# A sparse graph-attention layer: both adjacency searches together, GpSimd weights the own and row-aligned values, PE adds them

## The chip, the cores and the metric

The kernel runs on one core of a Trainium2 chip. The metric is the device time of one execution in microseconds (us), the median over runs. Before the change it is 662.41 us (3 runs, 660.38 to 662.70). A difference under about 0.5% (3.3 us) can't be told from no change. The engines are called PE (TensorE), DVE (VectorE), ACT (ScalarE), POOL (GpSimd) and SP (SyncE, which only issues transfers here).

## The reference

One layer of masked attention over N = 4096 rows of 256 features, 8 heads of 32, in float32, then a feed-forward block:

```python
mask = adj.astype(jnp.float32) + jnp.eye(n, dtype=jnp.float32)
q = (h @ Wq.T + bq).reshape(n, N_HEADS, D_K)      # k and v the same way
scores = jnp.einsum('nhd,mhd->hnm', q, k) / jnp.sqrt(jnp.float32(D_K))
scores = jnp.where(mask[None, :, :] == 0, jnp.float32(-1000000000.0), scores)
attn = jax.nn.softmax(scores, axis=-1)
ctx = jnp.einsum('hnm,mhd->nhd', attn, v).reshape(n, D_MODEL)
h1 = _layer_norm(h + ctx @ Wo.T + bo, ln1_g, ln1_b)
ff = jax.nn.relu(h1 @ W1.T + b1) @ W2.T + b2
return _layer_norm(h1 + ff, ln2_g, ln2_b)
```

`adj` is sparse, with few neighbours a row and more of them in the first tiles, so the kernel finds each row's neighbours and gathers only those. A second path (`general_*`), which is not run with these inputs, does the dense attention where a row has too many.

## The kernel before

The 4096 rows are 32 tiles of 128. A first phase (to about 98 us) projects keys and values into a table in HBM (`kv_table`) and starts on the queries. Then come 19 **steps**, numbered 0 to 18, in the order of `STEPS`. Steps 0 to 9, 17 and 18 take two tiles each (`q.T == 2`, one stretch of columns a tile, `q.nu == 1`). Steps 10 to 16 take one tile each, split into two or three stretches (`q.nu` 2 or 3). Tile 0, the densest, is done in pieces beside steps 2 to 14 (`TILE0`). Two steps make a group of four tiles (`place` 0 and 1), but steps 10 to 13 are one group and 14 to 16, with tile 0, another. The dense work of a group (output projection, feed-forward, both layer norms; `post_*`) runs one group later, spread over the gaps of the next group's steps.

A step works like this. DVE searches the adjacency rows of the step after the next with FIND_INDEX8 (`find_dve`, L492), once a tile. `listed_dve` and `spill_dve` (L505 to L533) turn what was found into lists. The first found column (or two) of a row is *row-aligned*: POOL gathers its key and value straight to that row's partition (L940). The rest are *edges*: PE and DVE sort them into shared chunks, and POOL gathers them (L948, and their queries, L952). A row's own key and value are loaded by SP. So each row has `q.own` slots in its own partition: 2 a tile in steps 0 to 5, 17 and 18, 3 in steps 6 to 9, 3 in steps 10 to 13 and 16, 4 in steps 14 and 15.

After the scores and the softmax (`norm_probs_dve`), the second half of a step has to be followed closely:

- DVE does the first search, takes a piece of tile 0 (L722), and subtracts the tops for the edges (`edge_below_dve`, L659).
- DVE multiplies the own and row-aligned values by their probabilities (L669 for two-tile steps, L672 and L675 for the others), and adds the slots into slot 0 (L682).
- DVE multiplies the edge values (`edge_weight_dve`, L688 and L691).
- PE sums into one PSUM bank (`sum_pe`): the edge chunks with a one-hot matrix (L822), and slot 0 with the identity (L823). ACT moves the result on (`ctx_act`), and the next group's projection (L998) waits for that.
- DVE does the second search (two-tile steps only), lists, spill, and at `place` 0 the second layer norm's statistics (L1083).

Each engine runs its own instructions in the order written; nothing is rescheduled. In that order PE's dense matmuls stand before and behind `sum_pe`, so whatever the sum waits for, they wait for too. At `place` 0, PE has the attention projection, then the queries of tile 0 (L835), and DVE's own piece of tile 0 (L702) waits for these.

Of the kernel before, what the change touches and what calls it, by code (L numbers as in the profile page):

```python
# [106 lines left out]
PIECES0 = TILE0.U // 2  # L107
SOFTMAX0 = SCORE0 + PIECES0
# [22 lines left out]
def build(nc, xT, adj, wqkvT, bq, bk, bqkv, woT, w1T, w2T, cols, g2, be2, out):  # L131
    with ExitStack() as ctx:
# [205 lines left out]
        own_sum = sem("own_sum")  # L338
        own_summed = sem("own_summed")
# [322 lines left out]
        def own_sum_dve(dve, q):  # L662
# [14 lines left out]
            dve.wait_ge(own_weighted, q.b + 1)  # L677
            done = total(lambda p: p.own - 1, q.b)
            v = slots[q.par][:, 0:q.T * q.own, D:].rearrange("p (t s) d -> p t s d", s=q.own)
            for a in range(1, q.own):  # L680
                wait(dve, own_sum, done + a - 1)
                nc.vector.tensor_tensor(v[:, :, 0, :], v[:, :, 0, :], v[:, :, a, :], ALU.add).then_inc(own_sum, 1)  # L682
# [125 lines left out]
        def sum_pe(pe, q):  # L808

            pe.wait_ge(edge_weighted, q.b + 1)  # L810
            wait(pe, own_sum, total(lambda p: p.own - 1, q.b + 1))
            pe.wait_ge(own_weighted, q.b + 1)
            wait(pe, ctx_ready, q.b)
            if q.b == SUM0 + 1:
                pe.wait_ge(ctx0_ready, 1)
            for ti in range(q.T):
                for k in range(KC):
                    to = ps[:, ACC, (k * 2 + ti) * P:(k * 2 + ti + 1) * P]
                    feats = slice(D + k * P, D + (k + 1) * P)
                    for u in range(q.nu):  # L820
                        c = ti * q.nu + u
                        nc.tensor.matmul(to, edge_slots(q)[:, c, feats], onehot[q.par][:, c, :], start=(u == 0), stop=False)  # L822
                    last = nc.tensor.matmul(to, own_slots(q, ti)[:, 0, feats], ident[:], start=False, stop=True)  # L823
            last.then_inc(acc_ps, 1)
# [79 lines left out]
        def ctx0_act(act):  # L904
# [4 lines left out]
            last.then_inc(ctx0_ready, 1)  # L909

# [449 lines left out]
        def _(pool):  # L1360
# [49 lines left out]
            for q in STEPS:  # L1410
# [11 lines left out]
                if soon:  # L1422
                    gather_edges(pool, soon)
                if 0 <= i - GATHER0 < PIECES0:
# [4 lines left out]
                if place == 1 and n >= 1:  # L1429

                    pool.wait_ge(edge_weighted, i + 1)
# [233 lines left out]
        def _(dve):  # L1665
# [42 lines left out]
            for q in STEPS:  # L1708
# [22 lines left out]
                if later:  # L1731
                    find_dve(dve, later, 0)
                if 0 <= i - SCORE0 < PIECES0:
# [6 lines left out]
                own_sum_dve(dve, q)  # L1740
# [5 lines left out]
                if later and later.T > 1:  # L1746
                    find_dve(dve, later, 1)
                if later:
# [55 lines left out]
```

## Time and profile before

| | before |
|---|---|
| median of 3 runs | 662.41 us |
| the profiled execution, its own time | 661.45 us |
| its span, first to last instruction | 659.4 us |
| PE busy (matmul) | 532.5 us, 81% |
| DVE busy | 477.9 us, 72% |
| POOL busy | 239.1 us, 36% |
| ACT busy | 169.6 us, 26% |
| mean granted clock of TensorE | 0.892 of 2.4 GHz |

The span leaves out 2.05 us around it (661.45 - 659.4). A PE row's duration is from issue to modelled end and matmuls overlap; the pace is read from start to start. "Idle before" names what ended an engine's wait, with its length.

### The profile page before, as it was taken

What the parts mean: (1) busy time and instruction counts of PE and PEld (TensorE: products, weight loads), DVE (VectorE), ACT (ScalarE), POOL (GpSimd) and SP (SyncE); (2) the same over time, 40 slices, a digit from 0 to 9 for tenths busy, and PEclk for the clock granted to TensorE, in tenths of its full rate; (3) what the DMA queues carried; (4) which work ended last, traced back from release to release, by engine and by line L of the source; (5) the groups of instructions that cost most, each with busy time, mean ns of one, the idle gap of its engine ahead of it and who ended that gap; (6) DMA issues with size and microseconds to landing.
All of it is one profiled execution on the core that took longest, in us unless ns stands there. A gap on an engine that the chain in (4) does not pass through costs nothing.

```text
span 659.4 us, 7652 instructions
## 1 busy us (share of the span) xinstructions
PE 532.5 (81%) x2434; PEld 423.7 (64%) x2434; DVE 477.9 (72%) x1210; ACT 169.6 (26%) x357; POOL 239.1 (36%) x370
## 2 busy tenths in 40 slices
PE   4999878884988897988889776588858489988891
PEld 3888667773577566747757652467755368577680
DVE  0798959869895997999779789989865996412000
ACT  1121312222421431342241242110314122521610
POOL 5010234454242373466424342424541424122222
PEclk9999778887899899889889986786959799999896
DMA  8999686997983888778562644347680843020100
GB/s 308 414 425 353 223 350 216 379 345 234 359 305 138 323 311 301 221 291 296 199 213 81 216 152 158 114 157 266 222 264 24 277 166 117 7 65 0 33 16 19
DMA packets 39211, 141.08 MB, mean 214 GB/s; under 512 B 4856, under 2 KB 15352, under 8 KB 35072
## 3 DMA queue, kind: packets, MB, share of 16 engines
q1 hardware_dynamic: 24320, 95.16, 39.1%
q0 software_dynamic: 13328, 43.55, 19.1%
q10 hardware_dynamic: 1520, 1.85, 0.8%
q8 instruction: 21, 0.34, 0.2%
q14 instruction: 22, 0.18, 0.1%
HBM read 123.74 MB, written 16.80 MB: 213 GB/s over the span
## 4 chain that ended last, share of the span: by engine, by line
PE 47%; DVE 29%; issue 8%; ACT 5%; DMA 5%; POOL 4%; POOLq 0%; SPq 0%; DVEq 0%; ACTq 0%
PE ps L1029 12%; PE ps L1017 12%; DVE found L492 7%; PE ps L1564 6%; PE ps L998 4%; DMA work<-q_table,row_of 4%; PE ps L988 3%; DVE stats L1083 2%; PE ps L822 2%; PE ps L823 2%; ACT early L1073 2%; ACT xT_all L1063 1%; DVE slots L682 1%; PE ps L864 1%; DMA xT_all<-in_xT 1%
## 5 line engine op out<-in xcount | busy, mean ns | idle before, releaser
L492 DVE FIND_INDEX8 found<-ones,adj_buf 128x8 uint32<-128x4105 int32 (+5 forms) x40 | 138.7, 3467 | 0.0
L1017 PE MATMUL ps<-xT_all,w 128*128 128x512 f32 (+1 forms) x288 | 129.6, 597 | 9.0 <-ACT xT_all L1063 7.9
L1029 PE MATMUL ps<-w,xT_all 128*128 128x256 f32 x512 | 123.7, 397 | 3.6 <-ACT xT_all L1063 3.1
L1029 PEld LDWEIGHTS ps<-w,xT_all 128*128 128x128 f32 x512 | 100.0, 200 | 18.2 <-ACT xT_all L1063 4.1
L1017 PEld LDWEIGHTS ps<-xT_all,w 128*128 128x128 f32 x288 | 57.3, 209 | 58.0 <-issue 45.0
L948 POOL DMA_INDIRECT slots<-kv_table,col_of x54 | 54.5, 1009 | 66.1 <-DVE col_of L566 54.5
L1083 DVE BATCH_NORM_STATS2 stats<-ps 128x6 f32<-128x256 f32 x64 | 22.9, 418 | 65.0 <-PE ps L988 65.0
L1564 PE MATMUL ps<-early,xT_all 128*128 128x256 f32 x256 | 59.1, 394 | 9.2 <-DMA xT_all<-in_xT 9.2
L1063 ACT ACTIVATE xT_all<-ps,col_table 128x512 f32<-128x512 f32 (+1 forms) x72 | 45.3, 641 | 71.3 <-PE ps L1017 66.8
L1564 PEld LDWEIGHTS ps<-early,xT_all 128*128 128x128 f32 x256 | 50.5, 199 | 16.5 <-issue 9.2
L822 PE MATMUL ps<-work,slots 128*128 128x128 f32 x160 | 35.5, 333 | 29.2 <-DVE slots L691 29.1
L940 POOL DMA_INDIRECT slots<-kv_table,found x32 | 33.6, 1051 | 56.8 <-PE ps L823 22.2
L1101 POOL TENSOR_TENSOR rstd<-mv,eps_col 128x4 f32<-128x4 f32 (+1 forms) x18 | 5.3, 297 | 132.5 <-DVE mv L1089 132.5
L822 PEld LDWEIGHTS ps<-work,slots 128*128 128x128 f32 x160 | 28.8, 238 | 33.4 <-DVE slots L691 33.4
L998 PE MATMUL ps<-wo,xT_all 128*128 128x256 f32 x128 | 36.8, 414 | 15.7 <-issue 12.4
L952 POOL DMA_INDIRECT work<-q_table,row_of x40 | 39.1, 978 | 12.2 <-issue 12.2
L892 ACT ACTIVATE xT_all<-ps,col_table 128x256 f32<-128x256 f32 (+1 forms) x38 | 14.4, 430 | 111.7 <-PE ps L823 111.7
L1582 PE MATMUL ps<-early,xT_all 128*128 128x256 f32 x128 | 38.0, 425 | 0.0
L1110 POOL TENSOR_TENSOR early<-early,row_g 128x1024 f32<-128x1024 f32 (+1 forms) x9 | 19.0, 2109 | 49.5 <-DVE slots L691 43.9
L998 PEld LDWEIGHTS ps<-wo,xT_all 128*128 128x128 f32 x128 | 24.0, 209 | 18.4 <-issue 16.2
L785 PE MATMUL ps<-idx_all,work 128*128 128x9 f32 (+1 forms) x80 | 12.9, 273 | 24.5 <-DVE work L547 24.5
L1582 PEld LDWEIGHTS ps<-early,xT_all 128*128 128x128 f32 x128 | 28.1, 219 | 5.0
(165 smaller groups left out, 881.3 us busy)
## 6 DMA issues: line engine op xcount, KB each, us to landing
adj_buf<-in_adj SPq DMA_DIRECT2D x31, 2048.0 KB
xT_all<-in_xT SPq DMA_DIRECT2D x15, 512.0 KB, 21.4
kv_table<-slots POOLq DMA_DIRECT2D x7, 1024.0 KB, 11.4
slots<-kv_table SPq DMA_DIRECT2D x12, 512.0 KB
q_table<-slots POOLq DMA_DIRECT2D x16, 256.0 KB, 9.5
out_dram<-early SPq DMA_DIRECT2D x7, 512.0 KB
q_own<-q_table SPq DMA_DIRECT2D x12, 256.0 KB
slots<-in_adj SPq DMA_DIRECT2D x1, 2048.0 KB, 24.5
```

The lines of the kernel that those rows point to most:

```text
L492: last = nc.vector.max_index(dst, ones8[:], part)
L822: nc.tensor.matmul(to, edge_slots(q)[:, c, feats], onehot[q.par][:, c, :], start=(u == 0), stop=False)
L940: nc.gpsimd.indirect_dma_start(to, None, kv_dram, bass.IndirectOffsetOnAxis(ap=idx, axis=0)).then_inc(got_aligned[q.par], 16)
L948: nc.gpsimd.indirect_dma_start(edge_slots(q)[:, u, :], None, kv_dram, bass.IndirectOffsetOnAxis(ap=col_of[q.par][:, u:u + 1], axis=0)).the ...
L952: nc.gpsimd.indirect_dma_start(q_edge[q.par][:, u, :], None, q_dram[q.no // 2], bass.IndirectOffsetOnAxis(ap=row_of[q.par][:, u:u + 1], ax ...
L998: nc.tensor.matmul(to, q["ctxT"][:, k, j * P:(j + 1) * P], wo[:, k, :], start=(k == 0), stop=False)
L1017: last = nc.tensor.matmul(ps[:, q["bank"] + f % 2, 0:q["g"] * P], w1[:, k, f * P:(f + 1) * P], q["h1T"][:, k, :], start=(k == 0), stop=(k ...
L1029: nc.tensor.matmul(to, q["ffT"][:, f, j * P:(j + 1) * P], w2[:, f, :], start=(f == 0), stop=False)
L1063: nc.scalar.activation(q["ffT"][:, f, :], ps[:, q["bank"] + f % 2, 0:q["g"] * P], ACT.Relu, bias=bias_1[:, f:f + 1]).then_inc(q["ff"], 1)
L1083: last = nc.vector.bn_stats(q["stats"][k][:, j, :], tile_out(q, q["bank"] + 2 * k, j))
L1564: last = nc.tensor.matmul(ps[:, kv_bank(i, part), j * D:(j + 1) * D], xT_all[:, c, k, r * P:(r + 1) * P], wqkv[:, k, (1 + part) * D:(2 + p ...
L1582: last = nc.tensor.matmul(to, xT_all[:, c, k, r * P:(r + 1) * P], wqkv[:, k, 0:D], start=False, stop=(k == KC - 1))
```

## The change

From step 2 on (`OWN_BY_POOL = 2`), the weighting of the own and row-aligned values moves from DVE to POOL (`own_weight_pool`), behind POOL's gathers for the next step and ahead of its gathers for tile 0. In all 19 steps the adding of the slots on DVE (L682) is gone: PE accumulates each slot with the identity, which makes `q.own` matmuls where there was one, for each tile and half of the features. In steps 2 to 18 DVE does the second search right behind the first, and the lists and spill ahead of the edge weighting, where they were behind it. POOL's gain and bias of the second layer norm (L1110, L1114) no longer wait for the step's edge weighting.

```diff
-        def own_sum_dve(dve, q):
+        def own_weight_dve(dve, q):
 ...
             last.then_inc(own_weighted, 1)
-            dve.wait_ge(own_weighted, q.b + 1)
-            done = total(lambda p: p.own - 1, q.b)
-            v = slots[q.par][:, 0:q.T * q.own, D:].rearrange("p (t s) d -> p t s d", s=q.own)
-            for a in range(1, q.own):
-                wait(dve, own_sum, done + a - 1)
-                nc.vector.tensor_tensor(v[:, :, 0, :], v[:, :, 0, :], v[:, :, a, :], ALU.add).then_inc(own_sum, 1)
 ...
             pe.wait_ge(edge_weighted, q.b + 1)
-            wait(pe, own_sum, total(lambda p: p.own - 1, q.b + 1))
             pe.wait_ge(own_weighted, q.b + 1)
 ...
-                    last = nc.tensor.matmul(to, own_slots(q, ti)[:, 0, feats], ident[:], start=False, stop=True)
+                    for a in range(q.own):
+                        last = nc.tensor.matmul(to, own_slots(q, ti)[:, a, feats], ident[:], start=False, stop=(a == q.own - 1))
 ...
+        def own_weight_pool(pool, q):
+
+            pool.wait_ge(own_probs, q.b + 1)
+            for ti in range(q.T):
+                v = own_slots(q, ti)[:, :, D:].rearrange("p s (h d) -> p s h d", d=DK)
+                if q.nu == 1:
+                    p = score_tiles(q)[:, ti, 0:q.own, :]
+                    last = nc.gpsimd.tensor_tensor(v, v, p.unsqueeze(3).to_broadcast([P, q.own, HEADS, DK]), ALU.mult)
 ...
+            last.then_inc(own_weighted, 1)
 ...
                 if soon:
                     gather_edges(pool, soon)
+                if i >= OWN_BY_POOL:
+                    own_weight_pool(pool, q)
 ...
                 if place == 1 and n >= 1:
-
-                    pool.wait_ge(edge_weighted, i + 1)
                     pool.wait_ge(s_weights, 16 * WEIGHT_DMAS)
 ...
                     find_dve(dve, later, 0)
+                if i >= OWN_BY_POOL and later and later.T > 1:
+                    find_dve(dve, later, 1)
 ...
                 edge_below_dve(dve, q)
-                own_sum_dve(dve, q)
+                if i < OWN_BY_POOL:
+                    own_weight_dve(dve, q)
+                elif later:
+                    listed_dve(dve, later)
+                    spill_dve(dve, later)
                 edge_weight_dve(dve, q)
 ...
-                if later and later.T > 1:
+                if i < OWN_BY_POOL and later and later.T > 1:
                     find_dve(dve, later, 1)
-                if later:
+                if i < OWN_BY_POOL and later:
                     listed_dve(dve, later)
                     spill_dve(dve, later)
```

On DVE, the second half of a two-tile step (step 3), before (MAX_INDEX is what the trace calls FIND_INDEX8; `adj_buf0` and `adj_buf1` hold the two tiles that are searched):

```order
L492 MAX_INDEX found<-ones8,adj_buf0 128x8
L659 TENSOR_TENSOR p_edge<-s_edge,ps 128x16
L669 TENSOR_TENSOR slots<-slots,scores 128x2x256 x2
L682 TENSOR_TENSOR slots<-slots 128x2x256
L688 SCALAR_TENSOR_TENSOR p_edge<-p_edge,ps 128x16
L691 TENSOR_TENSOR slots<-slots,p_edge 128x2x256
L492 MAX_INDEX found<-ones8,adj_buf1 128x8
L505 CAST idx_all<-found 128x2x8
L518 TENSOR_TENSOR mask1<-idx_all,limit 128x16
L520 TENSOR_REDUCE spill<-mask1 128x2
L526 SCALAR_TENSOR_TENSOR idx_all<-idx_all,row_ids 128x8 x2
L529 TENSOR_SCALAR half<-spill 128x2
```

and of the change, the same place:

```order
L492 MAX_INDEX found<-ones8,adj_buf0 128x8
L492 MAX_INDEX found<-ones8,adj_buf1 128x8
L659 TENSOR_TENSOR p_edge<-s_edge,ps 128x16
L505 CAST idx_all<-found 128x2x8
L518 TENSOR_TENSOR mask1<-idx_all,limit 128x16
L520 TENSOR_REDUCE spill<-mask1 128x2
L526 SCALAR_TENSOR_TENSOR idx_all<-idx_all,row_ids 128x8 x2
L529 TENSOR_SCALAR half<-spill 128x2
L531 SCALAR_TENSOR_TENSOR mask1<-idx_all,mask1 128x16
L533 TENSOR_SCALAR mask1<-mask1 128x16
L682 SCALAR_TENSOR_TENSOR p_edge<-p_edge,ps 128x16
L685 TENSOR_TENSOR slots<-slots,p_edge 128x2x256
```

The second search and the list work (L505 to L533) stand ahead of the edge weighting (L688 and L691, now L682 and L685); the own weighting and the adding are gone from DVE.

On POOL, step 5, from the gathers of the edges of step 6 to the next aligned gathers, before:

```order
L948 DMA slots<-kv_table,col_of 128x512
L952 DMA work<-q_table,row_of 128x256
L948 DMA slots<-kv_table,col_of 128x512
L952 DMA work<-q_table,row_of 128x256
L948 DMA slots<-kv_table,col_of 128x512 x2
L1110 TENSOR_TENSOR early<-early,row_g 128x1024
L1114 TENSOR_TENSOR early<-early,row_be 128x1024
L940 DMA slots<-kv_table,found 128x512 x4
```

and of the change:

```order
L960 DMA slots<-kv_table,col_of 128x512
L964 DMA work<-q_table,row_of 128x256
L960 DMA slots<-kv_table,col_of 128x512
L964 DMA work<-q_table,row_of 128x256
L914 TENSOR_TENSOR slots<-slots,scores 128x2x256 x2
L960 DMA slots<-kv_table,col_of 128x512 x2
L1122 TENSOR_TENSOR early<-early,row_g 128x1024
L1126 TENSOR_TENSOR early<-early,row_be 128x1024
L952 DMA slots<-kv_table,found 128x512 x4
```

Two multiplications (L914) stand between the next step's gathers and tile 0's, and the gain and bias are L1122 and L1126.

On PE, the sum of a step with three slots a tile (step 6), before:

```order
L822 MATMUL ps<-work,slots 128x128
L823 MATMUL ps<-ident,slots 128x128
L822 MATMUL ps<-work,slots 128x128
L823 MATMUL ps<-ident,slots 128x128
L822 MATMUL ps<-work,slots 128x128
L823 MATMUL ps<-ident,slots 128x128
L822 MATMUL ps<-work,slots 128x128
L823 MATMUL ps<-ident,slots 128x128
```

and of the change:

```order
L815 MATMUL ps<-work,slots 128x128
L817 MATMUL ps<-ident,slots 128x128 x3
L815 MATMUL ps<-work,slots 128x128
L817 MATMUL ps<-ident,slots 128x128 x3
L815 MATMUL ps<-work,slots 128x128
L817 MATMUL ps<-ident,slots 128x128 x3
L815 MATMUL ps<-work,slots 128x128
L817 MATMUL ps<-ident,slots 128x128 x3
```

One identity matmul becomes three for each tile and half.

## Rows read from the trace of the kernel before

**Rows 1.** the page: span, and the chain of waits by engine
```profile
span 659.4 us, 7652 instructions
PE 47%; DVE 29%; issue 8%; ACT 5%; DMA 5%; POOL 4%; POOLq 0%; SPq 0%; DVEq 0%; ACTq 0%
```

**Rows 2.** groups by line of PE (count | busy us, mean ns | idle before)
```profile
L822 PE MATMUL ps<-work,slots 128*128 128x128 f32 x160 | 35.5, 333 | 29.2 <-DVE slots L691 29.1
...
L823 PE MATMUL ps<-ident,slots 128*128 128x128 f32 x124 | 28.3, 316 | 0.0
...
L797 PE MATMUL ps<-work 128*128 128x56 f32 (+1 forms) x80 | 11.6, 271 | 3.1 <-DVE work L590 3.0
```

**Rows 3.** timeline of PE, steps 4 and 5 (start us, us, engine, line, operation, count, idle)
```profile
218.93 0.49 PE L822 MATMUL ps<-work,slots 128*128 128x128 f32 x2 [1.88 <-DVE slots L691]
...
248.10 0.39 PE L822 MATMUL ps<-work,slots 128*128 128x128 f32 x2
...
249.89 0.28 PE L778 MATMUL ps<-spill,minus_before 128*128 128x2 f32 x2
```

**Rows 4.** timeline of DVE, step 4, and step 5's last weighting
```profile
204.31 0.69 DVE L702 TENSOR_TENSOR slots<-ps,slots 128x512 f32<-128x512 f32 x1 [6.44 <-PE ps L835]
...
216.06 0.68 DVE L669 TENSOR_TENSOR slots<-slots,scores 128x512 f32<-128x512 f32 x1
...
217.38 0.69 DVE L682 TENSOR_TENSOR slots<-slots 128x512 f32<-128x512 f32 x1
...
218.87 4.43 DVE L492 FIND_INDEX8 found<-ones,adj_buf 128x8 uint32<-128x4105 int32 x1
...
224.51 0.42 DVE L1083 BATCH_NORM_STATS2 stats<-ps 128x6 f32<-128x256 f32 x1
...
242.90 0.69 DVE L691 TENSOR_TENSOR slots<-slots,p_edge 128x512 f32<-128x512 f32 x1
```

**Rows 5.** timeline of DVE, step 8: weighting and adding with three slots a tile
```profile
328.45 1.82 DVE L669 TENSOR_TENSOR slots<-slots,scores 128x768 f32<-128x768 f32 x2
...
330.30 1.42 DVE L682 TENSOR_TENSOR slots<-slots 128x512 f32<-128x512 f32 x2
```

**Rows 6.** timeline of PE: the sum's first matmul in steps 2, 8 and 15
```profile
164.44 0.58 PE L822 MATMUL ps<-work,slots 128*128 128x128 f32 x1 [4.56 <-DVE slots L691]
...
332.58 0.54 PE L822 MATMUL ps<-work,slots 128*128 128x128 f32 x1 [2.08 <-DVE slots L691]
...
516.35 0.58 PE L822 MATMUL ps<-work,slots 128*128 128x128 f32 x1 [5.00 <-DVE slots L691]
```

**Rows 7.** timeline of PE: waits behind a sum, steps 7, 12, 16
```profile
287.32 0.70 PE L1017 MATMUL ps<-xT_all,w 128*128 128x512 f32 x1 [2.34 <-ACT xT_all L1063]
...
426.44 0.50 PE L785 MATMUL ps<-idx_all,work 128*128 128x9 f32 x3 [1.85 <-DVE work L547]
...
521.65 0.38 PE L778 MATMUL ps<-spill,minus_before 128*128 128x2 f32 x2 [1.53 <-DVE spill L520]
...
526.48 0.50 PE L785 MATMUL ps<-idx_all,work 128*128 128x9 f32 x3 [1.85 <-DVE work L547]
```

**Rows 8.** one line's instructions (ns min/median/max, first and last start, forms): L1110, L511
```profile
L1110 POOL TENSOR_TENSOR early<-early,row_g x9: 1262/2350/2354, 243.7 to 648.1; 128x1024 f32<-128x1024 f32 x7, 128x512 f32<-128x512 f32 x2
...
L511 DVE CAST aligned_idx<-idx_all x7: 168/170/2341, 332.6 to 483.9; 128x2 uint32<-128x2 f32 x5, 128x3 uint32<-128x3 f32 x2
```

**Rows 9.** timeline of GpSimd: step 5's last gather, step 9's gain
```profile
241.33 0.95 POOL L948 DMA_INDIRECT slots<-kv_table,col_of  x1 [0.30 <-issue]
...
358.39 2.35 POOL L1110 TENSOR_TENSOR early<-early,row_g 128x1024 f32<-128x1024 f32 x1 [5.58 <-DVE slots L691]
```

**Rows 10.** timeline of DVE in step 9: the cast
```profile
358.43 2.34 DVE L511 CAST aligned_idx<-idx_all 128x2 uint32<-128x2 f32 x1
```

**Rows 11.** timelines at step 17: GpSimd's last gather, PE's first sum matmul
```profile
558.71 0.95 POOL L952 DMA_INDIRECT work<-q_table,row_of  x1 [0.30 <-issue]
...
560.54 0.39 PE L822 MATMUL ps<-work,slots 128*128 128x128 f32 x2
```

More of the change, by code:

```diff
@@ L107 @@
 PIECES0 = TILE0.U // 2
+OWN_BY_POOL = 2
 SOFTMAX0 = SCORE0 + PIECES0
@@ L337, in build @@
         own_weighted = sem("own_weighted")
-        own_sum = sem("own_sum")
-        own_summed = sem("own_summed")
         edge_weighted = sem("edge_weighted")
@@ L909, in ctx0_act @@
             last.then_inc(ctx0_ready, 1)
+        def own_weight_pool(pool, q):
[5 more added lines that the diff above has]
+                    last = nc.gpsimd.tensor_tensor(v, v, p.unsqueeze(3).to_broadcast([P, q.own, HEADS, DK]), ALU.mult)
+                else:
+                    p = score_tiles(q)[:, ti, 0:1, :]
+                    last = nc.gpsimd.tensor_tensor(v[:, 0:1], v[:, 0:1], p.unsqueeze(3).to_broadcast([P, 1, HEADS, DK]), ALU.mult)
+                    if q.A:
+                        p = unit_scores(q, 0, 1)[:, :, 0, :]
+                        last = nc.gpsimd.tensor_tensor(v[:, 1:], v[:, 1:], p.unsqueeze(3).to_broadcast([P, q.U, HEADS, DK]), ALU.mult)
+            last.then_inc(own_weighted, 1)
         def tables_ready(eng, q):
```

## The prediction

> **What bounds the kernel now.** I read the page first, then PE's groups by line, then the timelines of PE and DVE side by side, step by step. The chain of waits gives PE 47% and DVE 29% of a span of 659.4 us [rows 1]: two engines take turns. PE's sum is where they meet. Its first matmul follows 29.1 us of waiting for DVE's edge weighting, over 19 steps [rows 2], and its dense work is queued behind it. The reader is to see which steps hold that wait. They are the steps at place 0 (2, 4, 8 and 10) and three of the later, one-tile ones (11, 14, 15); four of them stand in [rows 3, 6]. At place 1 it is the other way round: in step 5 DVE has ended its weighting at 243.6 (242.90 + 0.69), and PE comes to the sum at 248.10 [rows 3, 4], 4.5 us of slack.
>
> So a pair of steps runs like this. From the end of a sum at place 1, PE goes through ctx and projection to L835; DVE waits 6.44 us for that, starts at 204.31, and has a fixed chain of its own up to the sum at 218.93. Then PE is full until 249.9. Work taken from DVE helps only inside that chain of 14.6 us. Elsewhere DVE would wait longer for PE.
>
> **The change part by part.** All sums are made against the profiled execution (661.45 us, of which 659.4 are the span and 2.05 lie around it). It stands 0.96 us under the median of 662.41.
>
> *PE's added matmuls.* One matmul in the program is two rows here: 124 rows of L823 for 62 calls [rows 2]. From 248.10 to 249.89 stand the 16 rows of one sum, 0.112 us each [rows 3]. The change adds 8 rows in a step with two tiles and two slots, 16 with two tiles and three slots (steps 6 to 9), 8 with one tile and three slots, 12 in steps 14 and 15. That is 192. The first 16 fall in steps 0 and 1, where the next step waits for gathers, and I count them nothing (if that cover is gone, 1.8 us). The other 176 by 0.112 are 19.7 us. They stand right behind the wait, ahead of everything that PE and ctx do next, in an engine that is full; I take all. The floor is half of it, if waits further on absorb the rest; the ceiling is twice it, 39 us, with the clock at the lower of its two levels (1.2 for 2.4 GHz) throughout.
>
> *The sum comes later where the second search is put ahead of it.* In step 4 the search and lists take from 218.87 to 224.51 (5.64, with its load 5.75) [rows 4]. What goes is the own weighting and adding, 216.06 to about 217.99 (1.93; the last add starts at 217.38). So the edge weighting ends 3.8 us later. In step 2 it is the same, in step 6, with three slots, the part that goes is 1.82 + 1.42 = 3.24 [rows 5], so 2.5 later, and in step 15 (four slots) about 3.1. These are steps where PE already waits for DVE or arrives with it (4.56, 1.88 and 5.00 us of waiting in 2, 4 and 15 [rows 3, 6]), so the delay goes straight on: 3.8 + 3.8 + 2.5 + 3.1 = 13.2 us. In steps 3, 5, 7 and 16 the 4.5 us of slack, as in step 5, hide it, with under 1 us left. The bounds of this term are 10 and 17.
>
> *GpSimd as the last.* POOL's price for a float32 product is not in this trace at these shapes with this broadcast. The nearest rows are 1.26 us for 512 elements and 2.35 for 1024 [rows 8]. I take 1.27 for 512, 1.8 for 768, 0.65 for 256. From below it is DVE's 0.69 for 512 [rows 4], from above twice the row. The work waits in POOL's order behind four to six gathers of 1.25 us each, and starts some 4 us after the probabilities. Beside two searches (9 us) that is hidden even at the upper price. Beside one it isn't: in steps 8, 10 and 14 DVE would reach the sum 1 to 2 us sooner, but POOL ends about when DVE ended before. And in step 17, where nothing is left to search, POOL's last gather ends at 559.66 and its products need 2.5 us more, against 560.54 for PE's sum [rows 11]: 1.6 us late.
>
> *The two engines hold each other up.* In step 9 the cast at 358.43 takes 2.34 us, beside GpSimd's gain (L1110), which starts at 358.39 and takes 2.35 [rows 9, 10]. Line L511 otherwise takes 0.17 [rows 8]. So small DVE work that falls beside a POOL product waits for its end, while the searches beside POOL are not slowed. With the wait on the edge weighting gone, the gain and bias in steps 5, 7, 9 and 15 start behind own weighting and tile 0's gathers. In step 5 the last gather is at 241.33 [rows 9]; 2.5 us more for the products, and gain and bias run from 245 to 250. DVE's lists now stand there, from 245.1 on, ahead of the edge weighting. It would end at about 251.2 where 247.4 was due, and PE's slack is gone: 2.9 us late. In steps 7, 9 and 15 the same arithmetic gives 0 to 2.8, 0 to 1.5 and 0 to 2.3, depending on tenths; I take 2.5 for the three. With steps 8, 10 and 14 (list work beside own weighting, 2.3 together, of 0 to 4) and step 17's 1.6 this term is 2.9 + 2.5 + 2.3 + 1.6 = 9.3 us, bounds 2 and 14.
>
> The Trainium skill ("SBUF — State Buffer", on the port pair that DVE and GpSimd share) says that a DVE instruction with two SBUF inputs, or in a two-port mode, and a GpSimd instruction that reads SBUF exclude each other for their full length. The trace agrees, with 2.34 against 0.17 us. By that rule edge weighting can also hold POOL up, 0.69 us at a time; the sum does not use this.
>
> *Given back.* With lists ahead of the sum, what DVE did between the sum and the next step is gone, and waits behind the sum close: L797's 3.0 us (steps 12 and 13 [rows 2]), 1.85 in step 12, 1.53 and 1.85 in step 16, and 2.34 in step 7, where the statistics now stand right behind the edge weighting [rows 7]. That is 10.6. Step 11, whose list work is shorter than the adding that goes, gives 0.8. Together 11.4 us; at least 6, at most 15.
>
> The sum: 19.7 + 13.2 + 9.3 - 11.4 = 30.8. 661.45 + 30.8 = 692.25; I predict **692 us**.
>
> **The rivals.**
>
> *GpSimd is hidden and the collisions don't happen.* The gain waits for the norm of ACT, which the later sum may delay, and then it would start beside PE's waiting and not beside the lists. For it: three of four collisions hang on tenths. Against it: the statistics stand earlier, so the norm is ready. Then 9.3 falls to about 1.6: 684.5 us.
>
> *GpSimd is much slower.* The product reads a broadcast in the innermost dimension, L1110 one in an outer. At twice the row, POOL's part in steps 8 to 10, 13, 14 and 17 grows by 3.6 or less each, 12 us together: 704 us. For it: no row has this form. Against it: nothing in the rows.
>
> *The searches wait for adjacency.* The second search is 7 us earlier against its own load. DVE never waits for it now. If it did by 3 us in four steps, it would be 704 as well.
>
> *Faster: DVE sets the pace.* If the chain of 29% on DVE were what bounds the pairs, the freed work (1.9 us in most steps, 3.2 in four) would shorten them. The point that decides is the sum's wait in steps 8, 10, 11 and 14: with GpSimd ready before DVE, each would shrink by up to 2 us, 6 to 8 together. For a faster kernel the added matmuls would also have to run in PE's waits, and the second search would have to be hidden in 2, 4 and 15. Then 661.45 - 7 = 654 us. Against it: PE waits only 1.88 us in step 4 and 4.56 in step 2, and DVE waits 6.44 for PE.
>
> *The delay is absorbed.* The change does what it says, but PE's extra rows and later sums vanish in waits: no change, 661 to 664.
>
> **How the numbers follow.** My forecast has 0.60 and its own range is 684 to 700. Hidden GpSimd has 0.20, slow GpSimd or late adjacency 0.14 together, absorbed 0.03, faster 0.03. The range of 8 in 10 takes in 684.5 and reaches down for the floor of the matmul term (9.9 less) and up toward 704: 674 to 704. About 0.5%, 3.3 us, can't be told from no change, and every case but the last two is far above it: slower 0.94, same 0.03, faster 0.03.
>
> **What would show it.** Right: PE's sum has 24 or 32 rows, with 0.112 us from one to the next at the full clock; the wait ahead of the sum in steps 2 and 4 grows by 3.8 us and more; DVE's wait at L835 grows beyond 6.44; L505 or L526 in step 5 takes about 2 us beside GpSimd's gain; DVE's busy time falls while the span grows. Wrong: PE's waits ahead of the sum stay as they were, products at GpSimd that take twice 1.27 us, a search that waits for its load, or a span under 674 us.

## The result and the profile after

| | before | changed |
|---|---|---|
| median, in one comparison on one chip | 662.56 us (4 runs) | 701.61 us (4 runs) |
| ratio | | 1.064, 95% interval 1.060 to 1.069 |
| the profiled execution, its span | 661.45, 659.4 us | 700.09, 698.3 us |
| granted clock of TensorE, mean of the span | 0.892 | 0.887 |

Slower, as forecast, but by 38.6 us from one profiled execution to the other where 30.8 were worked out, and by 6.4%, about 42 us, as the ratio has it. The median lies in the range of 674 to 704, and above the forecast's own 684 to 700; 662.41 times the ratio is 705, just above both.

The ratio is taken from fast executions only, side by side (one of the four before, at 667.24 us, was slow; without it their median is 662.41). It isn't the quotient of the medians, which is 1.059 here. In the runs below the two differ by up to 7 thousandths, 5 us, so a difference between two ratios is known to no better than that.

The page of the changed kernel: span, busy time and the chain of waits.

```profile
span 698.3 us, 7969 instructions
...
PE 557.4 (80%) x2626; PEld 450.6 (65%) x2626; DVE 454.3 (65%) x1144; ACT 169.3 (24%) x357; POOL 272.2 (39%) x404
...
PE 45%; DVE 35%; issue 6%; DMA 5%; ACT 4%; POOL 3%; SPq 0%; POOLq 0%; DVEq 0%; ACTq 0%
```

DVE's busy time fell from 477.9 to 454.3 us, and its share of the chain rose from the 29% of [rows 1] to 35%: less work, but more of it where PE waits. PE's groups by line (the sum is now L815 and L817) say the same:

```profile
L817 PE MATMUL ps<-ident,slots 128*128 128x128 f32 x316 | 55.6, 318 | 0.0
...
L815 PE MATMUL ps<-work,slots 128*128 128x128 f32 x160 | 35.9, 334 | 50.8 <-DVE slots L685 50.1
```

Against [rows 2], 192 rows came as counted (124 to 316), and the sum's wait for the edge weighting grew from 29.1 to 50.1 us. Step 4, DVE's timeline (start us, us):

```profile
211.38 0.69 DVE L696 TENSOR_TENSOR slots<-ps,slots 128x512 f32<-128x512 f32 x1 [5.68 <-PE ps L829]
...
218.52 4.43 DVE L492 FIND_INDEX8 found<-ones,adj_buf 128x8 uint32<-128x4105 int32 x1
...
222.93 4.43 DVE L492 FIND_INDEX8 found<-ones,adj_buf 128x8 uint32<-128x4105 int32 x1
...
229.05 0.69 DVE L685 TENSOR_TENSOR slots<-slots,p_edge 128x512 f32<-128x512 f32 x1
```

and PE's:

```profile
229.79 0.79 PE L815 MATMUL ps<-work,slots 128*128 128x128 f32 x2 [5.67 <-DVE slots L685]
```

From DVE's piece of tile 0 to the sum it is 18.41 us (211.38 to 229.79), where [rows 3, 4] had 14.62 (204.31 to 218.93): 3.8 us, the forecast to the tenth. DVE's own wait for L829 (L835 before) is 5.68 us, though, where the prediction named growth beyond 6.44 as a sign of being right. And in step 6, where 2.5 us and the rows' 1.8 were forecast, the kernel falls back by another 8.2, from 14.8 us behind at the end of step 5 to 23.0. Some 4.1 of them lie ahead of the sum. The rest is in the length of the sum itself. Step 6, the sum of the changed kernel:

```profile
288.74 0.61 PE L1000 MATMUL ps<-ident,early 128*128 128x128 f32 x4
293.42 0.79 PE L815 MATMUL ps<-work,slots 128*128 128x128 f32 x2 [4.07 <-DVE slots L685]
294.01 1.49 PE L817 MATMUL ps<-ident,slots 128*128 128x128 f32 x6
295.29 0.63 PE L815 MATMUL ps<-work,slots 128*128 128x128 f32 x2
295.71 1.49 PE L817 MATMUL ps<-ident,slots 128*128 128x128 f32 x6
...
299.53 3.60 PE L1029 MATMUL ps<-xT_all,w 128*128 128x512 f32 x8
```

Its 32 rows take 6.11 us (293.42 to 299.53), 0.19 us each, and not the 0.112 that stands in the prediction; before, its 16 rows took 1.89. The same stretch by windows (busy us of each engine with its rows, granted clock, DMA share, GB/s). The second row is the wait, the third the sum, the fourth the next projection:

```profile
core 0: us, PE busy (x) PEld busy (x) DVE busy (x) ACT busy (x) POOL busy (x), PEclk, DMA share, GB/s
...
274.00:289.00 15.00, 12.95 (x69) 11.51 (x68) 13.56 (x31) 2.25 (x5) 8.01 (x10) 0.89 0.27 65
289.40:293.40 4.00, 0.00 (x0) 0.00 (x0) 3.86 (x14) 1.55 (x3) 1.93 (x2) 0.79 0.98 406
293.40:299.50 6.10, 6.08 (x32) 6.08 (x33) 3.20 (x11) 0.00 (x0) 1.91 (x4) 0.58 0.99 418
299.50:306.00 6.50, 6.50 (x21) 3.49 (x20) 2.69 (x6) 4.36 (x9) 3.86 (x4) 1.00 0.85 306
```

PE stood idle for 4 us, the granted clock fell, and the sum ran at 0.58, most of it at 1.2 GHz. The next 6.5 us are at 2.4 GHz again. The Trainium skill ("TensorE: Matmul & The Clock Gate", on how the oscillation bites in real kernels) tells of this pattern: a wait for data lets the clock down, and the stage behind the wait starts at the low rate every time. The trace agrees here, 0.58 against 1.00, but not for "every time": in step 7 the sum's 32 rows take 5.30 us behind 3.13 us of waiting, and in a second trace of the same kernel (below) 3.68 us behind 3.16.

The collision of GpSimd with the lists in step 5, DVE:

```profile
256.53 1.50 DVE L505 CAST idx_all<-found 128x16 f32<-128x16 uint32 x1
...
258.35 2.26 DVE L526 SCALAR_TENSOR_TENSOR idx_all<-idx_all,row_ids 128x8 f32<-128x8 f32 x2
```

and POOL beside it:

```profile
251.14 2.06 POOL L914 TENSOR_TENSOR slots<-slots,scores 128x512 f32<-128x512 f32 x2
...
255.62 2.36 POOL L1122 TENSOR_TENSOR early<-early,row_g 128x1024 f32<-128x1024 f32 x1
258.06 2.38 POOL L1126 TENSOR_TENSOR early<-early,row_be 128x1024 f32<-128x1024 f32 x1
```

The cast ends about when L1122 ends (257.98), L526 about when L1126 does (260.44), as L511 did in [rows 9, 10]. 1.50 and 2.26 stand where 0.17 and 0.36 do in step 4, 3.2 us together.

### The profile page after: what moved, and what is told of

Its sections match the earlier page's. It is cut to its first block, busy times and chain, and to the rows that moved or that the text cites. A ratio compares the mean times of both kernels' runs of the same rounds, so it can differ in the third digit from the quotient of the medians.

```text
span 698.3 us, 7969 instructions
## 1 busy us (share of the span) xinstructions
PE 557.4 (80%) x2626; PEld 450.6 (65%) x2626; DVE 454.3 (65%) x1144; ACT 169.3 (24%) x357; POOL 272.2 (39%) x404
## 4 chain that ended last, share of the span: by engine, by line
PE 45%; DVE 35%; issue 6%; DMA 5%; ACT 4%; POOL 3%; SPq 0%; POOLq 0%; DVEq 0%; ACTq 0%
DVE found L492 13%; PE ps L1029 10%; PE ps L1041 7%; PE ps L1576 6%; PE ps L817 6%; PE ps L1010 5%; DMA work<-q_table,row_of 4%; PE ps L815 4%; PE ps L1000 3%; DVE stats L1095 2%; DVE slots L685 1%; DMA xT_all<-in_xT 1%; ACT early L1085 1%; POOL slots L960 1%; PE ps L858 1%
## 5 line engine op out<-in xcount | busy, mean ns | idle before, releaser
L1029 PE MATMUL ps<-xT_all,w 128*128 128x512 f32 (+1 forms) x288 | 126.8, 588 | 5.7 <-ACT xT_all L1075 4.6
L815 PE MATMUL ps<-work,slots 128*128 128x128 f32 x160 | 35.9, 334 | 50.8 <-DVE slots L685 50.1
L815 PEld LDWEIGHTS ps<-work,slots 128*128 128x128 f32 x160 | 29.1, 239 | 55.6 <-DVE slots L685 54.6
L952 POOL DMA_INDIRECT slots<-kv_table,found x32 | 33.2, 1037 | 79.9 <-PE ps L817 50.7
L1576 PEld LDWEIGHTS ps<-early,xT_all 128*128 128x128 f32 x256 | 50.5, 198 | 16.6 <-issue 9.3
L817 PE MATMUL ps<-ident,slots 128*128 128x128 f32 x316 | 55.6, 318 | 0.0
L1010 PE MATMUL ps<-wo,xT_all 128*128 128x256 f32 x128 | 40.9, 450 | 15.9 <-issue 10.2
L817 PEld LDWEIGHTS ps<-ident,slots 128*128 128x128 f32 x316 | 50.8, 235 | 0.0
L964 POOL DMA_INDIRECT work<-q_table,row_of x40 | 38.0, 950 | 12.2 <-issue 12.2
L1010 PEld LDWEIGHTS ps<-wo,xT_all 128*128 128x128 f32 x128 | 26.0, 225 | 19.1 <-issue 14.5
L539 DVE SCALAR_TENSOR_TENSOR bad<-spill,ps 128x2 f32<-128x2 f32 (+2 forms) x20 | 3.1, 154 | 52.5 <-PE ps L772 52.5
```

Source lines behind the costliest of these rows:

```text
L817: last = nc.tensor.matmul(to, own_slots(q, ti)[:, a, feats], ident[:], start=False, stop=(a == q.own - 1))
L964: nc.gpsimd.indirect_dma_start(q_edge[q.par][:, u, :], None, q_dram[q.no // 2], bass.IndirectOffsetOnAxis(ap=row_of[q.par][:, u:u + 1], ax ...
L1010: nc.tensor.matmul(to, q["ctxT"][:, k, j * P:(j + 1) * P], wo[:, k, :], start=(k == 0), stop=False)
L1029: last = nc.tensor.matmul(ps[:, q["bank"] + f % 2, 0:q["g"] * P], w1[:, k, f * P:(f + 1) * P], q["h1T"][:, k, :], start=(k == 0), stop=(k ...
L1576: last = nc.tensor.matmul(ps[:, kv_bank(i, part), j * D:(j + 1) * D], xT_all[:, c, k, r * P:(r + 1) * P], wqkv[:, k, (1 + part) * D:(2 + p ...
```

## The experiments

Each ran beside the kernel before on one chip; the ratio is to that, with its 95% interval. Beside it stands the lag, how much later than in the profiled kernel before PE began its first row behind a sum, from trace to trace (us). "Waits filled" means unread matmuls ahead of PE's waits; they come below.

| kernel | ratio | step 1 | 2 | 4 | 6 | 8 | 11 | 15 | 18 |
|---|---|---|---|---|---|---|---|---|---|
| changed | 1.064 | 4.3 | 8.2 | 12.9 | 23.0 | 29.1 | 34.7 | 37.0 | 40.0 |
| search behind | 1.008 | 5.0 | 4.7 | 4.8 | 6.2 | 5.5 | 7.9 | 5.4 | 5.5 |
| PE's added rows alone | 0.999 | 2.5 | 2.5 | 0.8 | 1.9 | -0.5 | 2.9 | -3.3 | -1.7 |
| order alone | 1.049 | -0.5 | 3.5 | 11.1 | 19.8 | 19.6 | 21.0 | 24.1 | 27.1 |
| order alone, waits filled | 1.030 | -0.3 | 2.2 | 8.1 | 15.0 | 12.9 | 12.8 | 15.7 | 20.1 |
| changed, waits filled | 1.028 | 4.5 | 6.8 | 9.6 | 17.4 | 20.2 | 20.8 | 23.6 | 25.4 |
| before, waits filled | 1.005 | -0.5 | -3.6 | -5.7 | -5.6 | -6.6 | -4.8 | -8.9 | -7.2 |
| all three taken away | 1.017 | -0.4 | 1.8 | 6.2 | 9.7 | 9.1 | 10.3 | 11.7 | 14.9 |

**PE's added rows alone.** The order of before, DVE weights, and PE adds the slots, in all steps. The edit is shown against the changed kernel.

```diff
-OWN_BY_POOL = 2
+OWN_BY_POOL = NB
+                    pool.wait_ge(edge_weighted, i + 1)     # gain
```

> The kernel before, but PE adds the slots (192 more matmul rows) and DVE no longer does; weighting, searches and the gain's wait stay where they were. Ledger theory (each term as in the prediction, waits absorb rows where PE waits for DVE): the rows cost their full 0.112 us each only in the steps where PE comes last (3, 5, 7, 9, 12, 13, 16 to 18), and nothing in steps where DVE's add (0.7 to 1.4 us) goes away ahead of the sum: about +12 us, 674. Rival, every added row lies on the path: +19.7 us, 682. Rival, the lower clock behind waits makes rows dearer than 0.112: over 682.

Measured: 657.77 us, 0.999 (0.994 to 1.003), at a clock of 0.926. The 19.7 us of the prediction are not there. DVE is rid of its adding, the sum's wait falls from 29.1 to 20.4 us,

```profile
L815 PE MATMUL ps<-work,slots 128*128 128x128 f32 x160 | 32.0, 305 | 20.4 <-DVE slots L685 20.4
```

and PE runs more of the time at its high level. So the rows are there and yet cost nothing: PE's busy time is 534.4 us for 532.5, although 192 rows by 0.112 are 21.5. The rest of its work got shorter by nearly as much. Two waits that the prediction took as given back by the order are gone here too, with the order of before: L797's 3.0 us in steps 12 and 13, and most of the 2.34 us in step 7 (0.56 are left).

**The order alone.** The kernel before with only the second search, lists and spill ahead of the edge weighting, from step 2 on.

```diff
+                if i >= 2 and later and later.T > 1:
+                    find_dve(dve, later, 1)
...
                 own_sum_dve(dve, q)
+                if i >= 2 and later:
+                    listed_dve(dve, later)
+                    spill_dve(dve, later)
```

> The kernel before with only the order of DVE changed from step 2 on: second search right behind the first, lists and spill ahead of the edge weighting; DVE still weights and adds, PE has no more rows. Ledger theory: the weighting ends 5.75 us later in steps 2, 4, 6 and 15, about 1.2 later in one-tile steps, 1 to 2 us over the slack in 3, 5 and 7, and 10 us are given back: about +20 us, 682. If the longer waits of PE also lower its granted clock: +24 or more, 686 to 692, with a mean clock under 0.887. Rival, the order is harmless and the rows of PE are all of the loss: 662.

Measured: 690.82 us, 1.049 (1.041 to 1.056). The order by itself costs about 31 us. From the end of one sum to the start of the next, steps 2, 4, 6 and 15 are 4.2, 5.7, 7.3 and 5.6 us longer in its trace than before, 22.7 together, close to 5.75 us for each search with its load. Steps 5, 7, 11, 12 and 16 are shorter, by 4.5 together, and steps 3, 8, 10, 13, 14 and 17 longer, by 6.8.

**The gain's wait back.** The changed kernel with GpSimd's gain and bias waiting for the edge weighting again.

```diff
                 if place == 1 and n >= 1:
+                    pool.wait_ge(edge_weighted, i + 1)
```

> The changed kernel with the wait of GpSimd's gain on the edge weighting put back. If the collisions of gain and bias with DVE's list work cost what they show in steps 5, 7, 9 and 15 (PE waits 2.29, 3.13, 0.92 us in the first three, L505 and L526 stretched to 1.50 and 2.26 us in step 5): L505 and L526 short again, and 6 to 8 us less, about 694 to 696. Rival, other work would have made PE wait anyway: under 2 us less, about 700.

Measured: 687.06 us, 1.042 (1.034 to 1.049), 23 thousandths (15 us) less than the changed kernel. In its trace PE doesn't wait at all for the sums of steps 5, 7 and 9 (2.29, 3.13 and 0.92 us in the changed kernel): the slack that the prediction counted on is there unless GpSimd's gain meets the lists.

**The search behind.** The changed kernel with second search, lists and spill behind the edge weighting.

```diff
-                if i >= OWN_BY_POOL and later and later.T > 1:
-                    find_dve(dve, later, 1)
...
-                elif later:
-                    listed_dve(dve, later)
-                    spill_dve(dve, later)
...
-                if i < OWN_BY_POOL and later:
+                if later:
```

> The changed kernel with the second search, lists and spill put back behind the edge weighting; GpSimd weights and PE adds as in the change. Ledger theory: the later sum (13 us), the collisions and the waits that lower the clock go; the 176 rows stay, and one-tile and no-search steps wait for GpSimd by a tenth to 1 us: about +17 to +20 us against the kernel before, 679 to 682. Rival, GpSimd's own weighting behind the gathers is late once one search stands beside it: PE waits 1 to 2 us more in each two-tile step, 695 or more.

Measured: 664.53 us, 1.008 (1.005 to 1.012). Rows, GpSimd's weighting and the free gain together cost 5 us, and by the table these arise in steps 0 and 1, where only PE's rows and the end of DVE's adding are new. All the rest hangs on the order.

**PE's waits filled.** Unread matmuls ahead of the sum's wait in nine steps: if the waits' own length were the price, this could only cost.

```diff
+FILL = {2: 14, 4: 10, 5: 4, 6: 8, 7: 6, 8: 2, 11: 10, 14: 14, 15: 14}
...
+        def keep_busy(count):
+            for _ in range(count):
+                nc.tensor.matmul(ps[:, ELL, 256:512], ident[:], w1[:, 0, 0:256], start=True, stop=True)
...
+            keep_busy(FILL.get(q.b, 0))
             pe.wait_ge(edge_weighted, q.b + 1)
```

> The changed kernel, with 2 to 14 matmuls of 256 columns (identity times a weight, into an unused half of a bank that nobody reads) ahead of the neighbor sum's wait in steps 2, 4 to 8, 11, 14 and 15, where PE waits 2 to 8 us. Theory of the clock: the long waits make PE slow afterwards (the sum of step 6 took 6.11 us where 1.89 stood before), so with the waits filled the sums of steps 4, 6 and 7 fall back by 2 to 4 us each, the mean granted clock rises from 0.887 to over 0.90, and the time falls by some 8 us, to 1.052 of the kernel before. Rival, the waits alone are the cost and the long sums only lie beside them: the clock rises, but the time stays at 1.06 or rises with the added matmuls.

Measured: 683.95 us, 1.028 (1.019 to 1.038), at 0.923. PE is busy 576.9 us for 557.4, and the kernel is 24 us faster by the ratio, 18 by the medians and 15 by the spans (683.2 for 698.3). Expected were 8. The sum of step 6, by PE's timeline:

```profile
285.92 3.62 PE L806 MATMUL ps<-w,ident 128*128 128x256 f32 x16
290.16 0.49 PE L822 MATMUL ps<-work,slots 128*128 128x128 f32 x2 [0.62 <-DVE slots L687]
290.49 0.83 PE L824 MATMUL ps<-ident,slots 128*128 128x128 f32 x6
...
293.84 3.60 PE L1036 MATMUL ps<-xT_all,w 128*128 128x512 f32 x8
```

and its window:

```profile
290.20:294.00 3.80, 3.80 (x33) 3.80 (x34) 3.14 (x11) 0.00 (x0) 1.91 (x4) 1.00 0.99 420
```

The same 32 rows take 3.68 us for 6.11, at a clock of 1.00 for 0.58. The transfers beside them are no rival for this: the DMA share is 0.99 in both. All 19 sums together take 66.8 us for 80.8 in the changed kernel (from first row to modelled end), and these 14 us are nearly all that the trace gains. L806 are the unread matmuls (eight in the program, 16 rows).

**The kernel before, filled.** The control: 3 to 12 unread matmuls in its seven waits.

> The kernel before, with unread matmuls of 256 columns ahead of the sum's wait where PE waits there (3 to 12 of them in steps 2, 4, 8, 10, 11, 14 and 15). Filling the changed kernel's waits moved it from 1.0644 to 1.0283. Theory that the change made new waits and so new time at the low level of the clock: the kernel before has less of both, and filling it gains some 0.5 to 1 %, 0.992. Rival, that filling gains the same in any order, so that the clock is no part of the change's price: 0.965.

Measured: 659.56 us, 1.005 (1.001 to 1.009). No gain, neither the rival's nor the 0.992 of the theory. By its time, then, what filling gives back in the changed kernel is the change's own price, and not something that any order would give. Its trace leaves some doubt: the wait ahead of the sum falls to 7.5 us, the 19 sums take 43.9 us for 55.4, and step 18 is 7.2 us ahead. But it is of the fastest of ten executions, 654.67 us, 4.9 below their median. By traces alone, up to 7 of the 15 us might be had in the order of before as well; by times none.

**The order alone, filled.** 2 to 18 unread matmuls in thirteen steps.

> The kernel with the change's order alone (both searches together, VectorE weights and adds, 1.0488 when measured), with 2 to 18 unread matmuls ahead of the sum's wait wherever PE waits there. Theory: of its 31 us some 20 are the search itself on the path and some 10 the clock after PE's waits: 1.03. Rival, all of it is VectorE's chain and the clock gives nothing back: 1.049.

Measured: 680.57 us, 1.030 (1.018 to 1.042). So of the order's 31 us some 12 are the clock (7 in the traces, 27.1 less 20.1), and some 20 stay with the clock held up. Both are rough: the quotient of the medians is 1.037.

**The changed kernel again**, for its ratio beside these.

> The changed kernel unchanged, beside the runs of this call, to have its ratio on the chip on which the others are compared: 1.06 by its first measurement. Should it come out at 1.045 to 1.05, the gain of the runs with the first steps as before and with filled waits is smaller than their ratios said.

Measured: 702.06 us, 1.064 (1.053 to 1.075), and every sum within 2.3 us of the first trace. The 1.064 stands.

**The first two steps as before.** DVE adds in steps 0 and 1, PE takes one identity matmul.

```diff
+            if q.b < OWN_BY_POOL:
+                pe.wait_ge(own_sum, q.b + 1)
...
+                    many = q.own if q.b >= OWN_BY_POOL else 1
```

> The changed kernel, with steps 0 and 1 as before the change: VectorE adds the two slots and PE takes one identity matmul of each feature half. Theory that the 16 added rows of those two steps make PE late there, and with it the copy, the store of q and the gather of step 1: the 4 us that the changed kernel has lost by the end of step 1 go, 1.058 of the kernel before. Rival, the 4 us come from the transfers and not from the rows: 1.064, no change.

Measured: 693.56 us, 1.044 (1.035 to 1.053), but only 3.3 us less by the profiled spans (695.0 and 698.3). The lag at the end of step 1 goes from 4.3 to 0.4 us. It arises at DVE's first product of step 1, which waits for the gathered queries. The changed kernel:

```profile
124.15 0.69 DVE L583 TENSOR_TENSOR work<-work,slots 128x512 f32<-128x512 f32 x1 [5.56 <-DMA work<-q_table,row_of]
```

and this one:

```profile
121.68 0.69 DVE L584 TENSOR_TENSOR work<-work,slots 128x512 f32<-128x512 f32 x1 [1.80 <-DMA work<-q_table,row_of]
```

GpSimd issued that gather (L964 in the changed kernel, L952 before) at the same time in the changed kernel and in the one before,

```profile
116.54 0.95 POOL L964 DMA_INDIRECT work<-q_table,row_of  x1 [0.30 <-issue]
```

and at 116.65 in the kernel before, where the product starts at 121.22. The gather isn't issued later, so what my expectation named, a copy, a store and a gather that come late behind PE's rows, isn't the way.

**The same kernel again.**

> The changed kernel with the first two steps as before the change, once more, since its medians gave 8 us and more and its profiled span 3.3. Theory that the trace is right: 1.058 to 1.060. Rival, that the medians are: 1.044.

Measured: 694.79 us, 1.057 (1.048 to 1.065), span 692.3. The interval holds the theory and not the rival. With the run above, the first two steps are worth 3 to 13 us; the product of step 1 starts at 120.81 here. Over all traces the two kinds keep apart: where DVE adds in steps 0 and 1 and PE takes one matmul, it starts at 119.67 to 121.68 (nine traces), where PE adds, at 122.80 to 126.14 (eight traces).

**PE's rows and an idle addition.** The changed kernel, with DVE's work of before in steps 0 and 1 and PE's rows of the change.

```diff
+            nc.vector.tensor_tensor(v[:, :, 0, :], v[:, :, 0, :], v[:, :, 0, :], ALU.max).then_inc(own_sum, 1)
```

> The changed kernel, where in steps 0 and 1 VectorE does an addition's worth of work again (the larger of slot 0 and slot 0, which changes nothing), while PE still adds both slots. It parts two causes of the lag of 4.3 us at the end of step 1. Theory: without the adding VectorE searches 0.9 us earlier, the next 2 MB adjacency load starts earlier, and the gather of queries lands 3 us later beside it; then the idle addition brings the first product of step 1 back to 121 to 122 us and the lag to 1 to 2 us (PE's rows, 0.9 each). Rival, PE's 16 rows and what follows from them: the lag stays at 4 us.

Measured: 693.52 us, 1.051 (1.045 to 1.057), span 698.3. Inconclusive: in the trace the product starts at 123.51, among those with PE's rows, and the lag at the end of step 1 is 4.6 us, as the rival has it, while the ratio is lower than the changed kernel's. The trace is of the slowest of six executions, 700.34 us. It speaks against the earlier search as the cause and for the rows, but by which way rows would delay the landing isn't shown.

**The gain freed in the kernel before.**

> The kernel before, with only GpSimd's wait on the edge weighting ahead of the hidden gain taken away. In the changed kernel that same freedom cost some 15 us (1.0644 against 1.0415 with the wait back). Theory that the collisions cost only where GpSimd's gain meets VectorE's list building ahead of the sum: here the lists stand ahead of the gain in any case, the gain runs beside the edge weighting instead of after it, and the two slow rows of steps 11 and 12 (2.34 us for the list row) go: 0.995, 3 us less. Rival, that the gain is dear wherever it runs beside VectorE: the edge weighting (fed from the same memory) gets longer, and the time rises by 3 to 10 us.

Measured: 666.66 us, 1.006 (1.001 to 1.011). Not faster, so the first theory fell. Its trace is 1 to 5 us ahead to step 4, and then it shows the rival's mechanism. GpSimd's bias and DVE's edge weighting in step 5:

```profile
240.09 2.68 POOL L1114 TENSOR_TENSOR early<-early,row_be 128x1024 f32<-128x1024 f32 x1
```

```profile
240.69 2.64 DVE L691 TENSOR_TENSOR slots<-slots,p_edge 128x512 f32<-128x512 f32 x1
```

That is 2.64 us for the 0.69 of [rows 4]. In step 7 the adding stands beside gain and bias (297.25 to 302.39):

```profile
297.31 5.63 DVE L682 TENSOR_TENSOR slots<-slots 128x512 f32<-128x512 f32 x2
```

It takes 5.63 us for the 1.42 of [rows 5]. DVE's second search and lists stand behind these, and PE, whose sums in steps 5 and 7 run at full pace (16 rows in about 2.0 us), then waits 3.04 and 2.98 us for DVE's spill (L520). Step 15's sum starts after 8.60 us of waiting, for 5.00.

**PE adds, waits filled.** The first kernel of this list with unread matmuls ahead of six sums and six projections.

> The kernel before, with PE adding the slots as the change has it (0.9985 of the kernel before in an earlier run), and 2 to 10 unread matmuls of 256 columns ahead of the sum's wait in steps 2, 4, 6, 11, 14, 15 and ahead of the attention projection in steps 4, 6, 8, 10, 14 and 17. Theory of the clock: PE's waits end in time at the low level of its clock; with them filled the clock goes from 0.926 to over 0.94 and the time to 0.985, about 650 us. Rival, that little of what runs at the low level is on the path: 0.998, no change.

Measured: 656.47 us, 0.988 (0.979 to 0.997). Near the theory; 5.7 us are lost in steps 0 and 1.

**The same with DVE adding in steps 0 and 1**, and fills that differ by up to two matmuls a step.

> The kernel before with PE adding the slots from step 2 on, VectorE adding in steps 0 and 1 as before, and unread matmuls ahead of the waits in seven steps and ahead of the attention projection in six. The same with PE adding in steps 0 and 1 too gave 0.9881 and had lost 5.7 us by the end of step 1. Theory that these come back in full: 0.981, about 649 us. Rival, that the slack of step 2 takes most of them, as in the kernel without filling: 0.987.

Measured: 649.44 us, 0.984 (0.974 to 0.994), at a clock of 0.940. The interval holds both expectations. It beats both kernels.

**Gain waits and waits filled**, the two edits above together, but with other fills: none in steps 5 and 7, some in 10 and 13, where the run above had none.

> The changed kernel with GpSimd's wait on the edge weighting back ahead of the hidden gain (1.0415 alone) and PE's waits filled with unread matmuls (1.0283 alone). If the two were separate prices, 23 and 36 thousandths, their sum would leave 1.005, less than the order filled by itself (1.030), which can't be. Theory that much of the freed gain's price is the clock after the waits that its collisions lengthen: the two together give 1.020 to 1.026, and the collisions themselves are worth 3 to 5 us. Rival, that they are separate: under 1.012.

Measured: 673.27 us, 1.018 (1.011 to 1.025). The two overlap: with the waits filled, the gain's wait is worth 10 thousandths, 7 us (12 by the spans, 671.0 and 683.2), and not 23. Its trace has the sum's wait at 7.9 us in all, where the one with waits filled alone left 12.9; so some of the 7 to 12 us can be the better fill.

**All three taken away:** these two, and DVE's adding in steps 0 and 1.

> The kernel just named, with VectorE adding in steps 0 and 1 as before the change too. What is left of the change is the search ahead of VectorE's scalar chain, the slots added by PE and GpSimd's weighting from step 2 on. Theory, the step by step ledger of the prediction without the clock: rows of PE cost nothing, the second search costs what it puts ahead of the sum less what GpSimd's weighting takes off VectorE, 8 to 12 us, 1.012 to 1.018. Rival, that the first steps' lag is worth nothing by itself: as the kernel just named.

Measured: 672.28 us, 1.017 (1.010 to 1.024). In the range of the theory; against the kernel just named the difference can't be told. In the traces that one ended step 1 at +2.8 and step 18 at +14.9, this one at -0.4 and +14.9.

## Why the prediction was right and wrong

Right was the direction, the place and the mechanism of the order. The wait ahead of the sum grew in steps 2 and 4 by 3.7 and 3.8 us (8.28 and 5.67 for the 4.56 and 1.88 of [rows 3, 6]). Step 5 collided as worked out, 2.3 us late for 2.9. GpSimd's products were hidden outside step 17, where the sum waits 0.69 us more for 1.6 forecast; they took 1.03 us for 512 elements (L914, 2.06 for two), under the 1.27 that I took from [rows 8]. One sign of being right failed: DVE's wait for the queries of tile 0 fell from 6.44 to 5.68 us.

The total in parts, once by ratios times 661.45 us (uncertain by some 5 us each), once from the traces at the end of step 18:

| | forecast | by ratios | by traces | from |
|---|---|---|---|---|
| rows, order and given back | 21.5 | 11 | 15 | left when all three are taken away |
| GpSimd's collisions (and steps 0, 1) | 9.3 | 8 | 10 | changed filled, less all three taken away |
| low clock after PE's waits | not counted | 24 | 15 | changed, less changed filled |
| sum | 30.8 | 42 | 40 | |

The fills of these kernels are not the same, which can shift some us between the first two rows. The first row is against the kernel before as it stands; against that kernel with its own waits filled, it is 8 us by ratios and 22 by traces.

The steps that failed:

1. *PE's added matmuls: "in an engine that is full; I take all"*, 19.7 us. 192 rows at 0.112 us, with the adding that they replace gone, cost nothing that can be measured, 0.999. The engine was full by count, with PE busy 81% and clock 0.892, but the wait ahead of the sum fell by 8.7 us, and PE's busy time rose by only 1.9: wait and clock gave back what the rows took. My floor was half. The true value was nothing.
2. *The price of a wait was its length.* The prediction used the two levels of the clock only as a ceiling for the rows, 39 us. The us that the order and the collisions added to PE's waits, from 29.1 to 50.1, cost more than themselves, since the sum behind them ran at the low level for much of its length: 15 to 24 us, at least as large as any other term, and not in the sum at all (the control leaves 7 as the least, by traces alone). The kernel before shows it. In step 8, behind the 2.08 us of waiting in [rows 6], PE's rows are

```profile
333.13 0.63 PE L823 MATMUL ps<-ident,slots 128*128 128x128 f32 x2
333.55 0.63 PE L822 MATMUL ps<-work,slots 128*128 128x128 f32 x2
...
336.10 3.60 PE L1017 MATMUL ps<-xT_all,w 128*128 128x512 f32 x8
```

and in step 9, without a wait,

```profile
361.10 0.39 PE L822 MATMUL ps<-work,slots 128*128 128x128 f32 x2
361.32 0.39 PE L823 MATMUL ps<-ident,slots 128*128 128x128 f32 x2
...
362.89 0.28 PE L778 MATMUL ps<-spill,minus_before 128*128 128x2 f32 x2
```

The same 16 rows take 3.52 us (332.58 to 336.10) there and 1.79 (361.10 to 362.89) here.
3. *Steps 0 and 1 "where the next step waits for gathers, and I count them nothing"*. 1.8 us were the price if the cover was gone; 4.3 was the lag at the end of step 1, and undoing the change there gave 3 to 13 us back.
4. *The second search ahead and what is given back*, in net 1.8 us without the rows. 11 to 15 were measured, with the rows at nothing. What failed is the 11.4 us given back. The order alone takes nothing off DVE, so its delay in steps 2, 4, 6 and 15 should be 5.75 each, 23.0, and its trace has 22.7. But 4.5 us are given back, under my least of 6, and 6.8 more are lost in steps that this term doesn't name. The waits that I took as given back go as well when only PE's rows are added, so a good part of them belonged to the rows, as the reason why these were free.

The errors, 20 us too much in the rows and 25 to 35 too little in clock and order, covered each other for the most part. That 692 comes close is luck.

Open are the clock's share, in all (7 to 24 us, by the yardstick) and step by step, since a fill can also lengthen a wait, and what in steps 0 and 1 makes the gathered queries land late.

## What to carry to other kernels

Where PE waits for another engine, price a longer wait by more than its length: read how long the first work behind a present wait takes against the same work without one (3.52 against 1.79 us here), and try it on each wait that the change makes. It is a risk and not a rate: behind the same wait, the sum of step 7 took 5.30 us in one trace of the changed kernel and 3.68 in the other. Added matmuls that take the place of a wait may be free, as 192 were here. And a bundle of edits is best timed in parts: all but the order together cost 0.8%, the order alone 5%.

## What the runs showed of the hardware

- Work that nobody reads made a kernel faster: 19.5 us more busy time on PE, 15 to 24 us less in all, with the clock from 0.887 to 0.923. In the kernel before, whose waits for the sum are 29.1 us, the same did nothing for the time (1.005).
- A wait of 4.07 us brought the granted clock to 0.58 over the next 6 us; filled down to 0.62 us of waiting it was 1.00.
- A GpSimd product of 512 float32 with a broadcast in its innermost dimension took 1.03 us, of 768 elements 1.46 (2.92 for two), less than the gain of before for 512 (1.26).
- A DVE product or addition beside a GpSimd product took 2.64 us for 0.69, and 5.63 for 1.42 (the kernel before with the gain freed); a cast 1.50 for 0.17.
